# Stage 3 of a six-stage decoder kernel: GpSimd adds four weighted values in two pairs, and the output projection takes four matmuls per chunk for six

## What is computed

```python
win = qkv[:, idx]                      # idx: windows of KS = 4 tokens, a start every ST = 2
q, k, v = jnp.split(win, 3, axis=-1)   # 8 heads of 16
dots = jnp.einsum('bnqhd,bnkhd->bnhqk', q, k) * scale
attn = jax.nn.softmax(dots, axis=-1)
o = jnp.einsum('bnhqk,bnkhd->bnqhd', attn, v)
y = o @ w_out + b_out
out = out.at[:, idx.reshape(-1), :].add(y.reshape(B, N * KS, C))
```

## Time and profile before

| | us |
|---|---|
| median of 3 runs | 759.81 |
| lowest, highest run | 751.41, 760.89 |
| the profiled execution, its own time | 763.6 |
| its span, first to last instruction | 761.7 |
| PE busy | 702.9 (92%) |
| DVE busy | 453.6 (60%) |
| ACT busy | 388.8 (51%) |
| POOL busy | 80.1 (11%) |
| mean granted TensorE clock | 0.973 |

### The profile page before, as it was taken

One profiled execution on the slowest core, in us unless ns is written; L12 is line 12 of the kernel. 1 busy time (PEld: TensorE's weight loads), 2 busy tenths in 40 slices (PEclk: granted clock), 3 DMA queues, 4 the chain that ended last, 5 costly groups with the idle time before them and its releaser, 6 DMA issues.

```text
span 761.7 us, 19881 instructions
## 1 busy us (share of the span) xinstructions
PE 702.9 (92%) x8362; PEld 362.5 (48%) x8362; DVE 453.6 (60%) x1115; ACT 388.8 (51%) x722; POOL 80.1 (11%) x83
## 2 busy tenths in 40 slices
PE   6899999997999968999988979999999899999996
PEld 3454545454555643444434444555655434444342
DVE  0664353634777776688466863666665566737772
ACT  2737374655676765334522323647564334554464
POOL 1381121211000000000002002112110000000000
PEclk9999999999999999999999988999999899999998
DMA  8400000000000005513500000000000000007430
GB/s 350 183 4 0 3 1 3 1 3 2 2 2 2 2 2 113 111 41 73 112 1 3 2 3 1 3 3 4 4 3 3 2 0 0 1 3 211 152 110 28
DMA packets 11639, 29.47 MB, mean 39 GB/s; under 512 B 1112, under 2 KB 1240, under 8 KB 11032
## 3 DMA queue, kind: packets, MB, share of 16 engines
q1 hardware_dynamic: 11552, 28.22, 12.7%
HBM read 26.97 MB, written 1.25 MB: 37 GB/s over the span
## 4 chain that ended last, share of the span: by engine, by line
PE 72%; DVE 11%; ACT 9%; issue 6%; DMA 2%; SPq 0%; DVEq 0%; ACTq 0%
PE banks L1812 5%; PE banks L2356 4%; PE banks L1843 4%; PE banks L2366 4%; PE banks L2056 3%; PE banks L2415 3%; PE banks L2044 3%; PE banks L2406 3%; PE banks L2131 3%; PE banks L2049 3%; PE banks L2191 3%; DVE sb_rowmax L1165 2%; PE banks L1856 2%; PE banks L2252 2%; PE banks L122 2%
## 5 line engine op out<-in xcount | busy, mean ns | idle before, releaser
L1812 PE MATMUL banks<-sb_xT,sb_arena 128*128 128x512 f32 x128 | 59.1, 610 | 6.5 <-DMA sb_arena<-w 6.5
L911 ACT ACTIVATE sb_arena<-banks 128x512 f32<-128x512 f32 x64 | 34.8, 606 | 48.0 <-PE banks L2222 48.0
L1502 DVE TENSOR_REDUCE sb_rowmax<-banks 128x4 f32<-128x512 f32 x64 | 41.2, 686 | 26.7 <-PE banks L2213 26.7
L641 ACT ACTIVATE sb_arena<-banks 128x512 f32<-128x512 f32 x64 | 36.1, 601 | 28.8 <-PE banks L1812 28.7
L817 ACT ACTIVATE sb_arena<-banks 128x512 f32<-128x512 f32 x36 | 21.5, 597 | 54.0 <-PE banks L2044 53.9
L1088 DVE TENSOR_TENSOR sb_arena<-banks,sb_arena 128x512 f32<-128x512 f32 x32 | 21.0, 687 | 46.0 <-PE banks L1856 46.0
L1812 PEld LDWEIGHTS banks<-sb_xT,sb_arena 128*128 128x128 f32 x128 | 24.8, 196 | 37.7 <-issue 36.0
L567 POOL TENSOR_TENSOR sb_arena<-sb_la,sb_consts 128x1024 f32<-128x1024 f32 x16 | 31.3, 1969 | 90.6 <-PE banks L1843 70.9
L2056 PE MATMUL banks<-sb_arena,sb_w 128*128 128x512 f32 x72 | 36.0, 600 | 2.3 <-DVE sb_arena L1387 2.3
L2044 PE MATMUL banks<-sb_xT,sb_w 128*128 128x512 f32 x72 | 38.0, 609 | 0.0
L2191 PE MATMUL banks<-sb_arena 32*64 32x512 f32 x256 | 35.9, 612 | 2.1 <-ACT sb_k_third L889 0.6
(11 more groups left out here) (327 smaller groups left out, 1513.8 us busy)
## 6 DMA issues: line engine op xcount, KB each, us to landing
sb_arena<-weights_by_expert SPq DMA_DIRECT2D x16, 512.0 KB, 7.8
sb_w<-weights_by_expert SPq DMA_DIRECT2D x32, 256.0 KB, 3.6
sb_w<-w SPq DMA_DIRECT2D x1, 2646.5 KB, 22.0
sb_w<-w SPq DMA_DIRECT2D x1, 1736.0 KB
sb_consts<-consts SPq DMA_DIRECT2D x1, 1227.0 KB, 10.5
sb_arena<-w SPq DMA_DIRECT2D x2, 512.0 KB, 5.7
sb_ctxT<-ctx SPq DMA_DIRECT2D x1, 1024.0 KB, 12.3
out<-sb_xT SPq DMA_DIRECT2D x4, 256.0 KB, 3.4
```

Of the source, the lines that this page charges most:

```text
L641: act.activation(BC[:, n, :], bank[(4, 5, 0, 1)[n % 4]][:], ACT.Copy).then_inc(s_vev, 1)
L911: act.activation(probT4[k % 2][:, g].rearrange("p b j q -> p (b j q)"), by_key[g][:], ACT.Exp).then_inc(s_e4, 1)
L1502: dve.tensor_reduce(rowmax4[k % 2][:, 4 * g:4 * g + 4], bank[n][:].rearrange("p (j t) -> p j t", j=4), AX, ALU.max).then_inc(s_mx4, 1)
L1812: pe.matmul(bank[(4, 5, 0, 1)[n % 4]][:], bc_w_tiles[:, n, :], cols(c), start=True, stop=True).then_inc(s_v, 1)
```

## The change

Two new SBUF tiles (`pair_sum`), a new semaphore, two additions per chunk on GpSimd at the end of its `front3`, and an output projection of four matmuls, which read the two sums and then `wv[:, 4]` and `wv[:, 5]`. TensorE's `project(0, 2)` now takes the two sums, and `project(2, 4)` the two single values.

```diff
+    pair_sum = [take(CHUNK) for _ in range(2)]
+    s_ps = sem("value_pairs_added")
...
                 pool.memset(vx4_all, 0.0).then_inc(s_z4, 1)
                 pool.memset(max4_all, 0.0).then_inc(s_z4, 1)
+            for n in range(2):
+                wait(pool, s_wv, 6 * c + 2 * n + 2)
+                wait(pool, s_po3, c)
+                pool.tensor_tensor(pair_sum[n], wv[:, 2 * n], wv[:, 2 * n + 1], ALU.add).then_inc(s_ps, 1)
...
                 for n in range(first, last):
-                    wait(pe, s_wv, 6 * c + n + 1)
-                    mm = pe.matmul(bank[7][:], w(3, "wo"), wv[:, n, :], start=(n == 0), stop=(n == 5))
-                if last == 6:
+                    if n < 2:
+                        wait(pe, s_ps, 2 * c + n + 1)
+                    else:
+                        wait(pe, s_wv, 6 * c + n + 3)
+                    mm = pe.matmul(bank[7][:], w(3, "wo"), pair_sum[n] if n < 2 else wv[:, n + 2, :], start=(n == 0), stop=(n == 3))
+                if last == 4:
                     mm.then_inc(s_po3, 1)
...
             project(0, 2)
             nxt(1)
-            project(2, 6)
+            project(2, 4)
```

## The result

The changed kernel takes 770.57 us (median of 4 runs, 767.28 to 772.47), the kernel before 760.35 (4 runs). The ratio is 1.015, 95% interval 1.009 to 1.021: slower by 10 us. The profiled execution took 770.75, its span 768.9, 7.2 us more than the span of before.

The account below looks back on a forecast made before the run. TensorE holds 72% of the chain of waits, but in stage 3 its removed matmuls stand beside the softmax. Chunk 0 +10.8, removed work -0.4, idle time at turns +2.6 make +13.0 on 759.8: 773 us, range 765 to 781.

Parts of the forecast that it names:

- What bounds the turn: Stage 3 turns: four matmuls and the softmax end together; line 2122 waits for line 1443, gain at most 0.2, taken as 0.
- The removed matmuls: Two matmuls per chunk from the second group, 6.9 us of TensorE: only -0.4 us, at stage 4's scores; bounds -0.4 to -6.9.
- The sums in the middle chunks: GpSimd's adds delay VectorE 1.3 us per chunk (0 to 2.2), within 1.9 us of slack: cost 0.
- Chunk 0: Sums stand behind line 144's wait and memsets on GpSimd; TensorE starts 8.8 us late, then half clock: +10.8, bounds +8.8 to +12.7.
- the 0.4 for the head sums: Chunk 0, line 2096's 192 small matmuls at half clock after the stall: +0.4 us, bounds 0 to 2.3.
- Idle time at the turns: New TensorE waits of some 1.7 us lower the clock at two of three turns: +2.6 us, bounds 0 to 4.3.
- The stall alone: Rival: chunk 0 stalls but the clock holds at the turns; +10.4 us, 770; chance 0.20.
- the case with cold turns: Main forecast: chunk 0's stall plus a lowered clock at some turns; +13.0 us, 773; chance 0.58.
- Columns count: Rival: TensorE's own queue holds line 2122, so each of three turns gains 1.7; +5.2 us, 765; chance 0.07.
- not slower: Rival: chunk 0's sums come in time, no stall; -0.4 us with warm turns, 759; chance 0.03.
- VectorE becomes the bound: Rival: two adds take more from VectorE than its 1.9 us slack, all turns cold; +15.9 us, 776; chance 0.12.

Follow-up runs that it names:

- The run with four values: Kernel before with weighted values 2 and 3 left out of the output projection and no sums anywhere; 759.83 us, ratio 0.999 to before.
- the reordered kernel: Changed kernel with chunk 0's sums ahead of x_bias3[3] and all four output matmuls behind the head sums, beside the softmax; 754.55 us, ratio 0.993 to before.
- The run with one pair: All output matmuls behind the head sums, only the first pair added on GpSimd, five output matmuls; 753.17 us, ratio 0.991 to before.
- the run with the memsets behind: Changed kernel with chunk 0's two sums behind x_bias3[3] but ahead of the two memsets for stage 4; 770.54 us, ratio 1.012 to before.
- sums early: Changed kernel with chunk 0's two sums moved ahead of x_bias3[3] in GpSimd's queue; 759.83 us against 762.70 of before, ratio 1.000.
- the run with early memsets: The run with one pair, with the two stage 4 memsets also moved ahead of x_bias3[3], behind chunk 0's sum; 753.78 us, ratio 0.992 to before.
- the runs with five matmuls: Two kernels with one pair's sum and five output matmuls behind the head sums, without and with the stage 4 memsets moved early; 753.17 and 753.78 us.

## Why the prediction was right, and where its terms were off

The forecast was 773, in a range of 765 to 781; measured are 770.57 and 770.33, with the stall, its cause and its place as forecast. The case that I thought most likely had a second part, a lower clock at the turns, and that part didn't happen.

*What bounds the turn.* Right: the softmax from the head sums to line 1443 sets it. With two matmuls less, line 2122 of before still starts 3.47 us after the group, with 1.49 us idle. The 0.2 that I called the most and took as 0 is 0.16 per turn. The run with four values shows it without any sum.

*The removed matmuls.* -0.4 forecast at the scores, 0.47 measured, and 3 x 0.16 at the turns: -0.9 in all, of 6.9 us of TensorE. I had no term for the gap in chunk 2's head sums, which all traces with four matmuls in this order lack: -0.7 here, if it belongs to the removal.

*The sums in the middle chunks.* Right in kind and size: the products took 1.07 longer (4.77 for 3.70), where I took 1.3 of 0 to 2.2. The first sum ran beside line 1462 and took nothing from it. But the slack wasn't the 1.9 us that I read in one chunk: 1.07 of it went to the products, and in chunk 2, where the head sums ran without their gap, 0.29 us was left. The rule that whoever comes second is blocked for the whole of the other is in the Trainium skill, "SBUF — State Buffer", "Who interferes with whom". The trace agrees for the one add that meets the products (1.07 lost to an add of 1.26). Both adds met them only in the reordered kernel, whose products took 5.86, 2.2 longer, and in no chunk of the changed one. The page also says that a VectorE instruction with at most one SBUF input doesn't contend with GpSimd, unless it runs in one of the modes that use two ports, and names the copy among those that can. The run with one pair agrees for the multiplication (products of 3.70), and the copy of 1.35 for 0.29 agrees with the exception.

*Chunk 0.* The start of the first matmul was forecast at 418.75 and came at 418.70; its end at half clock at 422.15, and line 2102 began at 422.38. Of the +10.8 the 0.4 for the head sums did not show in the difference: they took 2.2 us (422.38 to 424.59) as before (411.88 to 414.09). That is two things that cancel. The granted clock was 0.50 in their first us and 0.92 in the rest, and without a gap they took 2.21, while in the run with the memsets behind, at full clock and also without a gap, they took 1.76 (421.81 to 423.57): half clock cost some 0.45. Before, they had full clock and a gap of 0.24. Measured +10.1.

*Idle time at the turns.* This is the term that was wrong: 2.6 us, measured 0. I set 1.7 us of idle time against one case where 1.44 was followed by a low clock and one where 1.35 wasn't, and took the border to lie between. The idle time came out as 1.49 to 1.50, and in the five profiles that have such turns (the changed kernel twice, sums early, memsets behind, four values) none of 15 turns dropped the clock. One observation on either side gave no border, and the first of them repeats only in part: the same idle time of 1.44 us, ahead of the same matmuls, was followed by 0.50 in the changed kernel too (52.22 to 53.22), but by 1.00 in eight of the nine later traces (for one, 51.75 to 52.75 in the run with the sums early).

Without this term and the 0.4 the sum is +10.0, and the medians differ by 10.2. That they agree so closely is luck. Chunk 0 and what the removed matmuls gave make +9.35 in the trace (10.14 - 2 x 0.16 - 0.47), the spans differ by 7.2, and the interval is 7 to 16 us.

*The rivals.* "The stall alone" (+10.4, 770) is what happened; I gave it 0.20 and the case with cold turns 0.58. So the range held the result for the right cause, and the odds between the two cases were wrong. "Columns count" and "not slower" fell with the experiments. "VectorE becomes the bound" fell too, in chunk 2 by only 0.29 us.

## What to carry to other kernels

Work added to a nearly idle engine still stands in that engine's queue. Before placing it, list what is ahead of it and what the last of that waits for: here a bias whose release came 2.3 us after the sums were wanted, and a memset that only stage 4 needs. Removing work from the busiest engine pays only where nothing else ends at the same time; an engine that never idles can still be running beside the true bound, and the test is who releases the instruction behind the removed ones. Here both finds together, sums early and all output matmuls beside the softmax, turned a kernel 1.5% slower into one 0.7% faster (0.9% with one pair only, a difference that these runs don't resolve).

## What the runs showed of the hardware that was not expected

TensorE's idle times of 1.49 to 1.50 us at the turns never lowered the granted clock, while 1.44 us at 50.8 did in the kernel before and at 51.0 in the changed one, and in eight of the nine later traces did not. The wait of 2.73 us ahead of chunk 0's `spread(0)`, or 2.72, stands in all eleven traces: in five the projections behind it took 4.54 us, in six 2.84. The length of the idle time alone doesn't decide it, and the changed kernel's two traces show that the same program can go either way.

The same 192 head sums took from 1.8 us without a gap (451.27 to 453.04 in the changed kernel) to 3.1 with one of 1.08 us (416.92 to 419.98 in the run with early memsets). These gaps, "issue" in the trace, differ between chunks of one execution. In the old order the periods without a gap were 13.97 or 13.98, those with one 14.5 to 15.1. In chunk 2 that is about as much as the removed matmuls brought at all turns and at the scores together.

What causes the gaps wasn't tried. The traces give two signs. A gap stands nearly always at the same place of TensorE's program: in chunk 0 after 136 of the 192 in all four traces in the old order without a stall, in chunk 1 after 114 with six matmuls and after 118 with four. And in the three traces where TensorE had just waited 6 to 10 us for GpSimd, chunk 0 has none. That points at how TensorE's instructions reach it, more than at another engine. But it isn't the place alone: the runs with five matmuls, with the same program on TensorE, have a gap of 0.64 us in chunk 2 in one trace and none in the other.
